# The mesh product written as three products of high and low parts, with its loads moved to ScalarE and its loops written out

## The chip, the cores and the metric

The kernel runs on one core of one Trainium2 chip. The metric is the device time of the whole program in microseconds (us), the median of several runs.

## What is computed

A node array of 1250 x 512 passes through a three-layer graph network with a residual norm, then through an edge and node network with a second norm. The change touches only one product inside the second network. There the edge network multiplies, for every edge, the concatenation of an edge embedding, the mesh features of the source node and the grid features of the target node by one weight of 1536 x 512:

```
e_in = jnp.concatenate([e, mesh_nfeat[src], grid_nfeat[dst]], axis=-1)
e_new = _mlp(e_in, edge_W0, edge_b0, edge_W1, edge_b1, edge_g, edge_beta) + e
```

The kernel does the middle third once per node and not once per edge: it computes `mesh_nfeat[0:1250] @ edge_W0[512:1024]` up front, stores the 1250 x 512 result in a table in device memory (`mesh_table`), and the edge stage later gathers rows of that table.

## The kernel before

The program has three parts with a barrier between the first two: `phase_a` (the first 325 us of the profile), `phase_b` (the layers of the first network; the edge stage is nested in it) and `phase_d` (the last norm). Only `phase_a` is touched. It runs, on TensorE and in this order:

1. transposes and products of weights (`turn_weight`, `jobs`, the vectors of L761 to L770), to about 104 us;
2. the mesh product (L772 to L796): the 1250 rows are ten tiles of 125 rows. `turn` (L772) transposes a tile of `mesh` through the identity into PSUM bank 4 or 5, ScalarE's `mesh_copy` (L661) copies it to `mesh_t`, `multiply` (L780) multiplies it by the weight `w0b` in plain float32 into bank 6 or 7, VectorE's `mesh_copy` (L562) copies the result to `mesh_out`, and the DMA queue of SyncE (SP) stores it. All buffers are double. The order on TensorE is turn, turn, multiply, multiply for a pair of tiles, the first pair written out, the other four in a hardware loop;
3. the first layer's products (L798 to L830): each tile of `h` is turned (`turn_h`), split into a high part (ScalarE, `high`) and a low part (VectorE, `low`), and multiplied in `product` (L70) by two weights that are split in the same way. `product` takes, for each of four chunks, three matmuls of float32r operands: high by high, high by low, low by high;
4. counting of edges per pair of nodes with one-hot matrices (L832 to L855), in 176 steps. VectorE makes the one-hot matrices (L596, L597). Each step is released by a gate: SP opens the even ones and GpSimd (POOL) the odd ones (`open_gates`, L269), both of them after a first increment from TensorE's queue at L850.

Other queues beside the mesh product: SP loads mesh tile n+2 when tile n has been turned (L330), stores finished tiles (L333), then loads a bias (L339), waits for all scatters of GpSimd (L341), loads the sorted pairs (L342) and the next weights. GpSimd sends 72 small scatters (L391, L395) and then 24 of another kind (L145) before it enters `open_gates`. VectorE turns the pairs into numbers in the tile NB - 3 = 7 of the first layer (L623 to L627). ScalarE splits the first layer's weights into `w_hi` between the first mesh tiles (L672), and VectorE makes `w_lo` (L572).

Of the kernel before, what the change touches and what calls it, by code (L numbers as in the profile page):

```python
# [25 lines left out]
F32 = mybir.dt.float32  # L26
F32R = mybir.dt.float32r
# [3 lines left out]
ALU = mybir.AluOpType  # L31
ACT = mybir.ActivationFunctionType
# [3 lines left out]
P = 128  # L36
N = 1250
E = 21250
D = 512
A4 = 4  # L40
KC = D // P
NB = 10
NPB = N // NB
# [74 lines left out]

SORT_AT, TEMP_AT, FOLD_AT, SBUF_END = 87296, 112128, 132864, 229344  # L120
SUMS_AT, LATE_AT, AGG_AT, U_AT, SPARE_AT = 24768, 90624, 104192, 179968, 220928

# [35 lines left out]
def phase_a(nc, ctx, t, scratch, keep):  # L159

    sort, temp, hot, fold = (Region(nc, at, end) for at, end in (
        (SORT_AT, TEMP_AT), (TEMP_AT, FOLD_AT), (TEMP_AT, FOLD_AT), (FOLD_AT, SBUF_END)))
# [56 lines left out]
    w1t = [fd(f"w1t_{i}", [P, KC, D]) for i in range(2)]  # L219
    w1gt = [fd(f"w1gt_{i}", [P, KC, D]) for i in range(2)]  # L220
    w0a, wnb, w0b = (fd(n, [P, KC, D]) for n in ("w0a", "wnb", "w0b"))
    jobs_out = [fd(f"jobs_out{i}", [P, D]) for i in range(2)]
    rows_out = [fd(f"rows_out{i}", [3, D]) for i in range(2)]
    mesh = [fd(f"mesh{i}", [NPB, D]) for i in range(2)]
    mesh_t = [fd(f"mesh_t{i}", [P, KC, P]) for i in range(2)]
    mesh_out = [fd(f"mesh_out{i}", [NPB, D]) for i in range(2)]

    h, w = keep["h"], [keep["w0"], keep["w1"]]
    w_hi, w_lo, hc, ht_hi, ht_lo = ([keep[f"{n}{i}"] for i in range(2)] for n in ("w_hi", "w_lo", "hc", "ht_hi", "ht_lo"))
    bias0, u_hi, u_lo = keep["bias0"], keep["u_hi"], keep["u_lo"]  # L230
# [23 lines left out]
    mesh_in = [sem(f"mesh_in{i}") for i in range(2)]  # L254
    mesh_stored = [sem(f"mesh_stored{i}") for i in range(2)]
    mesh_turned, mesh_t_ok, mesh_mm, mesh_ok = (sem(n) for n in ("mesh_turned", "mesh_t_ok", "mesh_mm", "mesh_ok"))
    hot_ok = sem("hot_ok")
    count_mm = [sem(f"count_mm{b}") for b in range(3)]
    copied_out = [sem(f"copied_out{b}") for b in range(3)]
# [6 lines left out]
    def spread(b):  # L266
        return b[:].rearrange("p (k n) -> p k n", k=KC)[:, :, 0:NPB]
# [30 lines left out]
    def _(sp):  # L298
# [25 lines left out]
            for m, name in enumerate(vectors[r][0]):  # L324
                sp.dma_start(rows(scratch[name]), rows_out[r % 2][m:m + 1, :]).then_inc(job_out[r % 2], 16)

        with sp.Fori(0, NB // 2 - 1) as i:
            for u in range(2):
                sp.wait_ge(mesh_turned, 2 * i + u + 1)
                move_rows(sp, mesh[u][:], node_rows(t["L1_gnn_mesh_nfeat"], 2 * i + 2 + u), mesh_in[u])  # L330
            for u in range(2):
                sp.wait_ge(mesh_ok, 2 * i + u + 1)
                move_rows(sp, node_rows(scratch["mesh_table"], 2 * i + u), mesh_out[u][:], mesh_stored[u])  # L333
        for u in range(2):
            n = NB - 2 + u
            sp.wait_ge(mesh_ok, n + 1)
            move_rows(sp, node_rows(scratch["mesh_table"], n), mesh_out[u][:], mesh_stored[u])
# [68 lines left out]
    def _(dve):  # L406
# [155 lines left out]
        def mesh_copy(n, u, fixed):  # L562
            if not fixed:
                dve.wait_ge(mesh_stored[u], (n - u) * (MOVED // 2))
            dve.wait_ge(mesh_mm, n + 1)
            dve.tensor_copy(mesh_out[u][:], bank[6 + u][0:NPB, :]).then_inc(mesh_ok, 1)

        for u in range(2):
            mesh_copy(u, u, True)
        for i in range(2):  # L570
            dve.wait_ge(w_hi_ok, i + 1)
            dve.tensor_tensor(w_lo[i][:], w[i][:], w_hi[i][:].bitcast(F32), ALU.subtract).then_inc(w_lo_ok, 1)  # L572
        with dve.Fori(1, NB // 2) as i:
            for u in range(2):
                mesh_copy(2 * i + u, u, False)

        def low(n):
            u = n % 2
# [26 lines left out]
        for n in range(NB):  # L605
            u = n % 2
# [26 lines left out]
    def _(act):  # L633
# [21 lines left out]
        for r in range(len(vectors)):  # L655
            act.wait_ge(job_mm, NJ + r + 1)
            act.wait_ge(job_out[r % 2], rows_stored(r % 2, r))
            m = len(vectors[r][0])
            act.activation(rows_out[r % 2][0:m, :], bank[r % 2][0:m, :], ACT.Copy).then_inc(row_out_ok, 1)

        def mesh_copy(n, u, fixed):  # L661
            if not fixed:
                act.wait_ge(mesh_mm, n - 1)
            act.wait_ge(mesh_turned, n + 1)
            act.activation(mesh_t[u][:, :, 0:NPB],
                           bank[4 + u][:].rearrange("p (k n) -> p k n", k=KC)[:, :, 0:NPB], ACT.Copy).then_inc(mesh_t_ok, 1)

        for u in range(2):
            mesh_copy(u, u, True)
        act.wait_ge(next_in, MOVED + 32)  # L670
        for i in range(2):
            act.activation(w_hi[i][:], w[i][:], ACT.Copy).then_inc(w_hi_ok, 1)  # L672

        def copy_h(n):
            if n >= 2:
# [3 lines left out]
        for n in range(2):  # L679
            copy_h(n)  # L680

        with act.Fori(1, NB // 2) as i:
            for u in range(2):
                mesh_copy(2 * i + u, u, False)

        def high(n):
            act.wait_ge(hc_turned, n + 1)
# [24 lines left out]
    def _(pe):  # L712
# [59 lines left out]
        def turn(n, u, fixed):  # L772
            pe.wait_ge(mesh_in[u], MOVED if fixed else (n - u) * (MOVED // 2) + MOVED)
            if not fixed:
                pe.wait_ge(mesh_t_ok, n - 1)
            for c in range(KC):
                last = pe.transpose(bank[4 + u][:, c * P:c * P + NPB], mesh[u][:, c * P:(c + 1) * P], k["ident"][0:NPB, 0:NPB])
            last.then_inc(mesh_turned, 1)

        def multiply(n, u, fixed):  # L780
            pe.wait_ge(mesh_t_ok, n + 1)
            if not fixed:
                pe.wait_ge(mesh_ok, n - 1)
# [6 lines left out]
        for u in range(2):  # L790
            multiply(u, u, True)
        with pe.Fori(1, NB // 2) as i:
            for u in range(2):
                turn(2 * i + u, u, False)
            for u in range(2):
                multiply(2 * i + u, u, False)  # L796

        def turn_h(n):  # L798
            pe.wait_ge(hc_ok, n + 1)
# [81 lines left out]
def node_rows(matrix, n):  # L881
    return matrix[n * NPB:(n + 1) * NPB, :] if isinstance(n, int) else matrix[ds(n * NPB, NPB), :]
# [1366 lines left out]
```

## Time and profile before

| | us |
|---|---|
| median of 3 runs | 2269.05 (2267.54 to 2270.96) |
| profiled execution, its own time | 2268.53 |
| its span, first to last instruction | 2266.8 |
| TensorE busy in the span | 2191.7 |
| mean granted TensorE clock | 0.991 of full speed |

Times inside the profile are counted from the start of the span. An engine's row in a timeline gives the start, how long the merged group took, engine, line, operation, output and inputs, shape, how many instructions, and in brackets how long the engine was idle before and who ended that. "SPq", "POOLq" and "PEldq" are the instruction queues of those engines, where waits, increments and DMA issues are handled; a queue can be ahead of its engine. `b_w_hi`, `b_ht_hi` and the like are the first layer's high and low parts.

### The profile page before, as it was taken

The numbers are of one execution on the slowest core, as the hardware profiler recorded it, in microseconds if no ns is written. First come the engines' busy times: TensorE is split into PE (matmuls) and PEld (weight loads), VectorE is DVE, ScalarE is ACT, GpSimd is POOL, SyncE is SP. The second block draws the span as 40 slices with busy tenths as digits, with TensorE's granted clock in tenths as the row PEclk, the third lists the DMA queues.
The fourth block names the chain that finished last, engine by engine and source line by source line (L and its number), as shares of the span: only waits on it lengthen the run. The fifth ranks groups of instructions, "written<-read, shape, count | busy, mean of one in ns | idle before, by whom it ended". The sixth has DMA issues, their size and how long they took to land. (4 is left out here: it accounts for less than half of the span.)

```text
span 2266.8 us, 44871 instructions
## 1 busy us (share of the span) xinstructions
PE 2191.7 (97%) x13036; PEld 1880.9 (83%) x13040; DVE 1502.4 (66%) x3372; ACT 1217.2 (54%) x2244; POOL 1207.9 (53%) x1725
## 2 busy tenths in 40 slices
PE   6999989999999999999999999999999999999898
PEld 4358877777789989989899898998989989889776
DVE  8325985343856776677767767667676776766666
ACT  1211114242346667666676677666767667667421
POOL 1785018884525555555555555555555565555223
PEclk9999999999999999999999999999999999999899
DMA  8231001112364333333233333333333323333131
GB/s 243 67 74 41 0 5 40 8 40 52 89 192 121 64 63 64 60 65 63 58 65 65 63 62 64 61 65 62 63 60 65 65 60 62 63 62 63 29 92 45
DMA packets 80400, 149.80 MB, mean 66 GB/s; under 512 B 20247, under 2 KB 20713, under 8 KB 80341
## 3 DMA queue, kind: packets, MB, share of 16 engines
q0 software_dynamic: 48464, 98.04, 22.7%
q1 hardware_dynamic: 31877, 51.01, 7.1%
q8 instruction: 33, 0.54, 0.1%
q14 instruction: 26, 0.21, 0.0%
HBM read 128.90 MB, written 19.71 MB: 66 GB/s over the span
## 5 line engine op out<-in xcount | busy, mean ns | idle before, releaser
L1655 ACT ACTIVATE b_bank<-c_bias 128x512 f32<-128x512 f32 x528 | 316.4, 599 | 15.1 <-PE b_bank L1767 5.2
L145 POOL DMA_INDIRECT s_attrs<-k_attrs,k_row_i x170 | 224.2, 1319 | 168.5 <-POOLq L2221 117.7
L1588 DVE CUSTOM_DVE_ANT_0 b_bank<-b_bank,c_p,k_floor 128x512 f32<-128x512 f32 x176 | 132.5, 753 | 255.6 <-PE b_bank L1789 254.7
L1433 POOL DMA_INDIRECT c_from_src<-s_dst_table,c_at_nodes x173 | 278.6, 1611 | 31.5 <-issue 31.5
L1844 PE MATMUL b_bank<-k_m_hi,c_pt_hi 128*128 128x512 f32 x704 | 293.8, 417 | 0.0
L1420 POOL DMA_INDIRECT c_from_src<-s_mesh_table,c_at_nodes x176 | 202.0, 1148 | 156.3 <-POOL c_at_nodes L1416 143.1
L1845 PE MATMUL b_bank<-k_m_lo,c_pt_hi 128*128 128x512 f32 x704 | 278.0, 395 | 0.0
L1846 PE MATMUL b_bank<-k_m_hi,c_pt_lo 128*128 128x512 f32 x704 | 273.9, 389 | 0.0
L1439 POOL TENSOR_TENSOR c_dev<-c_var,k_half 128x1 f32<-128x1 f32 x176 | 98.6, 560 | 327.4 <-DVE c_var L1570 327.4
L1726 ACT ACTIVATE c_h<-c_from_src 128x512 f32<-128x512 f32 x176 | 111.3, 632 | 263.4 <-DVE c_from_src L1609 263.4
L1787 PE MATMUL b_bank<-c_m_hi,c_ht_hi 128*128 128x384 f32 x704 | 222.5, 316 | 6.3 <-DVE c_ht_lo L1575 6.0
L1787 PE MATMUL b_bank<-k_m_hi,c_pt_hi 128*128 128x384 f32 x704 | 224.7, 319 | 0.0
L1789 PE MATMUL b_bank<-c_m_hi,c_ht_lo 128*128 128x384 f32 x704 | 218.6, 311 | 0.0
L1788 PE MATMUL b_bank<-c_m_lo,c_ht_hi 128*128 128x384 f32 x704 | 217.8, 309 | 0.0
L1789 PE MATMUL b_bank<-k_m_hi,c_pt_lo 128*128 128x384 f32 x704 | 217.1, 308 | 0.0
L1788 PE MATMUL b_bank<-k_m_lo,c_pt_hi 128*128 128x384 f32 x704 | 216.9, 308 | 0.0
L1604 DVE SCALAR_TENSOR_TENSOR c_rp_lo<-c_p,c_dev,c_rp_hi 128x512 fp32r<-128x512 f32 x176 | 132.3, 751 | 74.1 <-ACT c_rp_hi L1718 71.8
L1846 PEld LDWEIGHTS b_bank<-k_m_hi,c_pt_lo 128*128 128x128 f32 x704 | 132.8, 189 | 32.3
L1718 ACT ACTIVATE c_rp_hi<-c_p,c_dev 128x512 fp32r<-128x512 f32 x176 | 127.7, 726 | 55.0 <-POOL c_dev L1455 54.9
L1651 ACT ACTIVATE c_p<-b_bank 128x512 f32<-128x512 f32 x176 | 105.6, 600 | 92.4 <-PE b_bank L1764 91.8
L1844 PEld LDWEIGHTS b_bank<-k_m_hi,c_pt_hi 128*128 128x128 f32 x704 | 132.4, 188 | 23.9
L1455 POOL TENSOR_TENSOR c_dev<-c_var,k_half 128x1 f32<-128x1 f32 x176 | 130.1, 739 | 41.0 <-DVE c_var L1591 35.6
(355 smaller groups left out, 5862.8 us busy)
## 6 DMA issues: line engine op xcount, KB each, us to landing
c_from_src<-s_mesh_table,c_at_nodes POOLq DMA_INDIRECT x176
c_from_src<-s_dst_table,c_at_nodes POOLq DMA_INDIRECT x173, 4.7
s_attrs<-k_attrs,k_row_i POOLq DMA_INDIRECT x170
a_mesh<-in_L_gnn_mesh_nfeat_dram SPq DMA_DIRECT2D x10, 224.0 KB
k_h<-in_x_dram POOLq DMA_DIRECT2D x1, 2240.0 KB
s_mesh_table<-a_mesh_out SPq DMA_DIRECT2D x10, 224.0 KB
b_x<-in_x_dram SPq DMA_DIRECT2D x10, 224.0 KB
s_node_own<-b_out SPq DMA_DIRECT2D x10, 224.0 KB
```

What stands on the lines that cost most here:

```text
L145: return pool.indirect_dma_start(scratch["attrs"], bass.IndirectOffsetOnAxis(ap=k["row_i"][0:EP, c:c + 1], axis=0), k["attrs"][0:EP, A4 * ...
L1420: pool.indirect_dma_start(from_src[u][:], None, scratch["mesh_table"], bass.IndirectOffsetOnAxis(ap=at_nodes[u][:, 0:1], axis=0)).then_inc ...
L1433: pool.indirect_dma_start(from_src[u][:], None, scratch["dst_head" if head else "dst_table"], bass.IndirectOffsetOnAxis(ap=at_nodes[u][:, ...
L1588: dve.tensor_tensor_reduce(var1_bank[:], var1_bank[:], p[u % 2][:], 1.0 / D, k["floor"][:, 0:1], ALU.mult, ALU.add, var[u][:, 0:1]).then_i ...
L1604: dve.scalar_tensor_tensor(out=rp_lo[u][:], in0=p[u % 2][:], scalar=dev[u][:, 0:1], in1=rp_hi[u][:].bitcast(F32), op0=ALU.mult, op1=ALU.su ...
L1655: act.activation(bank[:], bias[:, m, :], ACT.Copy).then_inc(bank_set, 1)
L1787: pe.matmul(to, left[0][:, c, :], high, start=False, stop=False, skip_group_check=True)
L1788: pe.matmul(to, left[0][:, c, :], low, start=False, stop=False, skip_group_check=True)
L1789: last = pe.matmul(to, left[1][:, c, :], high, start=False, stop=(c == KC - 1), skip_group_check=True)
L1844: pe.matmul(edge_bank[:], left[0], m_hi[1][:, c, :], start=False, stop=False, skip_group_check=True)
L1845: pe.matmul(edge_bank[:], left[0], m_lo[1][:, c, :], start=False, stop=False, skip_group_check=True)
L1846: last = pe.matmul(edge_bank[:], left[1], m_hi[1][:, c, :], start=False, stop=(c == KC - 1), skip_group_check=True)
```

## The change

- `mesh_t` becomes float32r. `w0b` is split into `w0b_hi` (ScalarE, after the second vector) and `w0b_lo` (VectorE), and each turned tile gets a low part `mesh_lo` (VectorE, `mesh_low`). `w0b_hi` lies where `w0a` was, `w0b_lo` over `w0b` itself, `mesh_lo` over `wnb`.
- `multiply` uses `product`: twelve matmuls of float32r operands for a tile in place of float32 matmuls of four chunks.
- The order on TensorE becomes turn 0, turn 1, then for each n: multiply n, turn n+2, all of it written out.
- Mesh tiles 2 to 9 are loaded from ScalarE's queue (`mesh_load`), behind the copy of tile n-2. SP only stores.
- `w_hi` and `w_lo` are made between other tiles than before: ScalarE's `w_hi` behind the loads of tiles 3 and 4, VectorE's `w_lo` behind tiles 2 and 4.

```diff
-    mesh_t = [fd(f"mesh_t{i}", [P, KC, P]) for i in range(2)]
+    mesh_t = [fd(f"mesh_t{i}", [P, KC, P], F32R) for i in range(2)]
...
-        with sp.Fori(0, NB // 2 - 1) as i:
-            for u in range(2):
-                sp.wait_ge(mesh_turned, 2 * i + u + 1)
-                move_rows(sp, mesh[u][:], node_rows(t["L1_gnn_mesh_nfeat"], 2 * i + 2 + u), mesh_in[u])
-            for u in range(2):
-                sp.wait_ge(mesh_ok, 2 * i + u + 1)
-                move_rows(sp, node_rows(scratch["mesh_table"], 2 * i + u), mesh_out[u][:], mesh_stored[u])
...
+        for n in range(NB):
             sp.wait_ge(mesh_ok, n + 1)
+            move_rows(sp, node_rows(scratch["mesh_table"], n), mesh_out[n % 2][:], mesh_stored[n % 2])
...
+        def mesh_low(n, u, fixed):
+            dve.wait_ge(mesh_t_ok, n + 1)
+            if not fixed:
+                dve.wait_ge(mesh_mm, n - 1)
+            dve.tensor_tensor(mesh_lo[u][:, :, 0:NPB], spread(bank[4 + u]), mesh_t[u][:, :, 0:NPB].bitcast(F32),
+                              ALU.subtract).then_inc(mesh_lo_ok, 1)
+
+        dve.wait_ge(w0b_hi_ok, 1)
+        dve.tensor_tensor(w0b_lo[:], w0b[:], w0b_hi[:].bitcast(F32), ALU.subtract).then_inc(w0b_ok, 1)
         for u in range(2):
+            mesh_low(u, u, True)
+        for n in range(NB):
+            mesh_copy(n, n % 2, n < 2)
+            if n + 2 < NB:
+                mesh_low(n + 2, n % 2, False)
+            if n in (2, 4):
+                i = n // 2 - 1
+                dve.wait_ge(w_hi_ok, i + 1)
+                dve.tensor_tensor(w_lo[i][:], w[i][:], w_hi[i][:].bitcast(F32), ALU.subtract).then_inc(w_lo_ok, 1)
...
+            if r == 1:
+                act.activation(w0b_hi[:], w0b[:], ACT.Copy).then_inc(w0b_hi_ok, 1)
...
+        def mesh_load(n):
+            act.wait_ge(mesh_turned, n - 1)
+            move_rows(act, mesh[n % 2][:], node_rows(t["L1_gnn_mesh_nfeat"], n), mesh_in[n % 2])
+
         for u in range(2):
             mesh_copy(u, u, True)
+            mesh_load(2 + u)
         act.wait_ge(next_in, MOVED + 32)
         for i in range(2):
             act.activation(w_hi[i][:], w[i][:], ACT.Copy).then_inc(w_hi_ok, 1)
+            mesh_copy(2 + i, i, False)
+            mesh_load(4 + i)
...
+        for n in range(4, NB):
+            mesh_copy(n, n % 2, False)
+            if n + 2 < NB:
+                mesh_load(n + 2)
...
         def turn(n, u, fixed):
             pe.wait_ge(mesh_in[u], MOVED if fixed else (n - u) * (MOVED // 2) + MOVED)
             if not fixed:
-                pe.wait_ge(mesh_t_ok, n - 1)
+                pe.wait_ge(mesh_lo_ok, n - 1)
...
         def multiply(n, u, fixed):
-            pe.wait_ge(mesh_t_ok, n + 1)
-            if not fixed:
+            pe.wait_ge(mesh_lo_ok, n + 1)
+            if fixed:
+                pe.wait_ge(w0b_ok, 1)
+            else:
                 pe.wait_ge(mesh_ok, n - 1)
-            for c in range(KC):
-                last = pe.matmul(bank[6 + u][0:NPB, :], mesh_t[u][:, c, 0:NPB], w0b[:, c, :], start=(c == 0), stop=(c == KC - 1))
-            last.then_inc(mesh_mm, 1)
+            left = (lambda c: mesh_t[u][:, c, 0:NPB], lambda c: mesh_lo[u][:, c, 0:NPB])
+            product(pe, bank[6 + u][0:NPB, :], left, (lambda c: w0b_hi[:, c, :], lambda c: w0b_lo[:, c, :]),
+                    range(KC)).then_inc(mesh_mm, 1)
 
         for u in range(2):
             turn(u, u, True)
+        for n in range(NB):
+            multiply(n, n % 2, n < 2)
+            if n + 2 < NB:
+                turn(n + 2, n % 2, False)
```

## Rows read from the trace of the kernel before

**Rows 1.** Busy time by stretch: PE, PEld, DVE, ACT, POOL; clock, DMA share, GB/s.

```profile
104.00:145.20 41.20, 39.93 (x121) 19.24 (x121) 10.54 (x11) 10.55 (x15) 33.36 (x26) 1.00 0.43 108
207.20:323.60 116.40, 110.23 (x1939) 104.33 (x1938) 111.26 (x346) 13.78 (x38) 2.11 (x2) 1.00 0.01 1
```

**Rows 2.** TensorE's timeline, the mesh product and the start of the first layer.

```profile
103.95 1.07 PE L777 MATMUL a_bank<-k_ident,a_mesh 125*128 125x125 f32 x8
105.28 7.13 PE L785 MATMUL a_bank<-a_w0b,a_mesh_t 128*125 128x512 f32 x16 [0.26 <-issue]
112.25 1.02 PE L777 MATMUL a_bank<-k_ident,a_mesh 125*128 125x125 f32 x8
...
145.21 1.02 PE L803 MATMUL a_bank<-k_ident,b_hc 125*128 125x125 f32 x8
147.20 0.49 PE L73 MATMUL a_bank<-b_w_hi,b_ht_hi 128*125 128x512 f32 x1 [0.97 <-DVE b_ht_lo L582]
```

**Rows 3.** TensorE's timeline, one tile of the first layer (24 product matmuls, then a turn).

```profile
153.24 0.48 PE L73 MATMUL a_bank<-b_w_hi,b_ht_hi 128*125 128x512 f32 x1
...
158.45 0.39 PE L74 MATMUL a_bank<-b_w_lo,b_ht_hi 128*125 128x512 f32 x1
158.69 0.40 PE L75 MATMUL a_bank<-b_w_hi,b_ht_lo 128*125 128x512 f32 x1
...
159.27 0.48 PE L73 MATMUL a_bank<-b_w_hi,b_ht_hi 128*125 128x512 f32 x1
```

**Rows 4.** ScalarE's timeline around the mesh product.

```profile
97.19 0.59 ACT L659 ACTIVATE a_rows_out<-a_bank 2x512 f32<-2x512 f32 x1 [2.85 <-PE a_bank L769]
...
104.63 1.07 ACT L665 ACTIVATE a_mesh_t<-a_bank 128x500 f32<-128x500 f32 x2
105.58 3.71 ACT L672 ACTIVATE b_w_hi<-k_w 128x2048 fp32r<-128x2048 f32 x2
```

**Rows 5.** VectorE's timeline around the mesh product and in the first layer.

```profile
109.01 0.69 DVE L566 COPY a_mesh_out<-a_bank 125x512 f32<-125x512 f32 x1 [30.25 <-PE a_bank L785]
113.06 4.48 DVE L572 TENSOR_TENSOR b_w_lo<-k_w,b_w_hi 128x2048 fp32r<-128x2048 f32 x2
146.47 0.68 DVE L582 TENSOR_TENSOR b_ht_lo<-a_bank,b_ht_hi 128x500 fp32r<-128x500 f32 x1 [0.36 <-ACT b_ht_hi L690]
196.52 0.28 DVE L624 TENSOR_SCALAR a_pair_src<-a_pair_i 88x256 int32<-88x256 int32 x1
```

**Rows 6.** DMA issues on SP (ns min/median/max), then KB and us to landing.

```profile
L875 SPq DMA_DIRECT2D a_mesh<-in_L_gnn_mesh_nfeat_dram x20: 311/329/1922, 13.8 to 133.0; - x20
...
b_bias<-in_L_gnn_bs_dram SPq DMA_DIRECT2D x1, 256.0 KB, 3.8
a_w<-in_L_gnn_emb_W_dram SPq DMA_DIRECT2D x1, 1024.0 KB, 5.5
```

**Rows 7.** DMA traffic from 105.87 to 109.87 us, GB/s in 40 slices of 0.1 us.

```profile
GB/s 0 22 7 23 0 0 0 0 0 102 61 184 102 123 184 328 410 410 389 209 51 31 87 84 225 184 164 164 164 328 307 287 229 235 85 22 28 7 0 0
```

**Rows 8.** GpSimd's timeline while VectorE made w_lo.

```profile
111.67 1.18 POOL L391 DMA_INDIRECT s_pairs<-a_sort_pay,a_chunk_row  x1 [0.30 <-issue]
113.16 3.25 POOL L391 DMA_INDIRECT s_pairs<-a_sort_pay,a_chunk_row  x1 [0.30 <-issue]
116.71 1.89 POOL L391 DMA_INDIRECT s_pairs<-a_sort_pay,a_chunk_row  x1 [0.30 <-issue]
```

**Rows 9.** What can hold the count: pair load on SP, queues at the gates.

```profile
175.09 0.29 SPq L342 DMA_DIRECT2D a_pair_i<-s_pairs  x1
...
L273 POOLq MOVE  x1: 29/29/29, 191.7 to 191.7; - x1
...
L850 PEldq EVENT_SEMAPHORE  x3: 51/51/51, 204.4 to 204.7; - x3
```

**Rows 10.** Stretches in which the granted clock was low (columns as in the first group).

```profile
325.70:332.40 6.70, 3.59 (x9) 2.85 (x10) 2.12 (x9) 2.54 (x2) 4.13 (x4) 0.50 0.06 1
...
2254.00:2258.00 4.00, 3.84 (x10) 3.07 (x11) 2.29 (x5) 0.00 (x0) 2.53 (x3) 0.57 0.01 3
```

More of the change, by code:

```diff
@@ L120 @@
 SORT_AT, TEMP_AT, FOLD_AT, SBUF_END = 87296, 112128, 132864, 229344
+W0A_AT, WNB_AT, W0B_AT = (FOLD_AT + n * KC * D * 4 for n in (6, 7, 8))
 SUMS_AT, LATE_AT, AGG_AT, U_AT, SPARE_AT = 24768, 90624, 104192, 179968, 220928
@@ L221, in phase_a @@
     w0a, wnb, w0b = (fd(n, [P, KC, D]) for n in ("w0a", "wnb", "w0b"))
+    assert fold.at == W0B_AT + KC * D * 4
     jobs_out = [fd(f"jobs_out{i}", [P, D]) for i in range(2)]
@@ L224, in phase_a @@
     mesh = [fd(f"mesh{i}", [NPB, D]) for i in range(2)]
-    mesh_t = [fd(f"mesh_t{i}", [P, KC, P]) for i in range(2)]
+    mesh_t = [fd(f"mesh_t{i}", [P, KC, P], F32R) for i in range(2)]
     mesh_out = [fd(f"mesh_out{i}", [NPB, D]) for i in range(2)]
+    w0b_hi = Region(nc, W0A_AT, SBUF_END)("a_w0b_hi", [P, KC, D], F32R)
+    w0b_lo = Region(nc, W0B_AT, SBUF_END)("a_w0b_lo", [P, KC, D], F32R)
+    late_low = Region(nc, WNB_AT, SBUF_END)
+    mesh_lo = [late_low(f"a_mesh_lo{i}", [P, KC, P], F32R) for i in range(2)]
     h, w = keep["h"], [keep["w0"], keep["w1"]]
@@ L256, in phase_a @@
     mesh_turned, mesh_t_ok, mesh_mm, mesh_ok = (sem(n) for n in ("mesh_turned", "mesh_t_ok", "mesh_mm", "mesh_ok"))
+    w0b_hi_ok, w0b_ok, mesh_lo_ok = sem("w0b_hi_ok"), sem("w0b_ok"), sem("mesh_lo_ok")
     hot_ok = sem("hot_ok")
@@ L325, in _ @@
                 sp.dma_start(rows(scratch[name]), rows_out[r % 2][m:m + 1, :]).then_inc(job_out[r % 2], 16)
-        with sp.Fori(0, NB // 2 - 1) as i:
-            for u in range(2):
-                sp.wait_ge(mesh_turned, 2 * i + u + 1)
-                move_rows(sp, mesh[u][:], node_rows(t["L1_gnn_mesh_nfeat"], 2 * i + 2 + u), mesh_in[u])
-            for u in range(2):
-                sp.wait_ge(mesh_ok, 2 * i + u + 1)
-                move_rows(sp, node_rows(scratch["mesh_table"], 2 * i + u), mesh_out[u][:], mesh_stored[u])
-        for u in range(2):
-            n = NB - 2 + u
+        for n in range(NB):
             sp.wait_ge(mesh_ok, n + 1)
-            move_rows(sp, node_rows(scratch["mesh_table"], n), mesh_out[u][:], mesh_stored[u])
+            move_rows(sp, node_rows(scratch["mesh_table"], n), mesh_out[n % 2][:], mesh_stored[n % 2])
         sp.dma_start(bias0[:], rows(t["L0_gnn_bs"][0]).broadcast_to([P, D])).then_inc(bias_in, 16)
@@ L566, in mesh_copy @@
             dve.tensor_copy(mesh_out[u][:], bank[6 + u][0:NPB, :]).then_inc(mesh_ok, 1)
-        for u in range(2):
[L569 to L575, printed above, removed]
+        def mesh_low(n, u, fixed):
[6 more added lines that the diff above has]
+        dve.tensor_tensor(w0b_lo[:], w0b[:], w0b_hi[:].bitcast(F32), ALU.subtract).then_inc(w0b_ok, 1)
+        for u in range(2):
+            mesh_low(u, u, True)
[7 more added lines that the diff above has]
+                dve.tensor_tensor(w_lo[i][:], w[i][:], w_hi[i][:].bitcast(F32), ALU.subtract).then_inc(w_lo_ok, 1)
         def low(n):
@@ L680, in _ @@
             copy_h(n)
-        with act.Fori(1, NB // 2) as i:
-            for u in range(2):
-                mesh_copy(2 * i + u, u, False)
+        for n in range(4, NB):
+            mesh_copy(n, n % 2, False)
+            if n + 2 < NB:
+                mesh_load(n + 2)
         def high(n):
@@ L780, in multiply @@
         def multiply(n, u, fixed):
-            pe.wait_ge(mesh_t_ok, n + 1)
-            if not fixed:
+            pe.wait_ge(mesh_lo_ok, n + 1)
+            if fixed:
+                pe.wait_ge(w0b_ok, 1)
+            else:
                 pe.wait_ge(mesh_ok, n - 1)
-            for c in range(KC):
-                last = pe.matmul(bank[6 + u][0:NPB, :], mesh_t[u][:, c, 0:NPB], w0b[:, c, :], start=(c == 0), stop=(c == KC - 1))
-            last.then_inc(mesh_mm, 1)
+            left = (lambda c: mesh_t[u][:, c, 0:NPB], lambda c: mesh_lo[u][:, c, 0:NPB])
+            product(pe, bank[6 + u][0:NPB, :], left, (lambda c: w0b_hi[:, c, :], lambda c: w0b_lo[:, c, :]),
+                    range(KC)).then_inc(mesh_mm, 1)
         for u in range(2):
             turn(u, u, True)
[L790 to L796, printed above, removed]
+        for n in range(NB):
+            multiply(n, n % 2, n < 2)
+            if n + 2 < NB:
+                turn(n + 2, n % 2, False)
         def turn_h(n):
```

## The prediction

> **What bounds the kernel now.** I read the busy time by stretch first, because a share over the whole span hides which stage a change touches. The mesh stage lasts 41.2 us, of which TensorE is busy 39.93, and it is not busy with anything else [rows 1]. VectorE and ScalarE are busy about 10.5 us each, GpSimd 33.4 us with scatters that are not needed here. So TensorE's own work ends this stage. The timeline of TensorE says how it is spent: a pair of tiles repeats every 8.24 us (103.95 to 112.25 is the first, with four more behind it, to 145.21), of which two turns take about 1.0 and sixteen float32 matmuls 7.0; the idle time is 0.26 us a pair, one wait for the copy of the turned tile [rows 2]. The whole stage is 145.21 - 103.95 = 41.26 us. The chain of waits on the page reaches back only into the last part of the program, so it says nothing of this stage; what matters is what stands behind it. Behind it TensorE goes on at once with the first layer [rows 2], and it is busy 97% of the whole span. The queues are in order and the second part begins behind a barrier, so time taken out here is kept if no other queue has a date of its own before that barrier.
>
> **The change, part by part.**
>
> *The product.* Twelve float32r matmuls of 128*125 by 128x512 replace eight float32 ones. The first layer runs just this form: a tile there starts at 153.24 and the next at 159.27, 6.03 us for 24 matmuls and a turn; two neighbours start 0.233 us apart (158.45 to 158.69, rounded) [rows 3]. So 24 matmuls are 5.60 and a turn with its changes of form is 6.03 - 5.60 = 0.43. A mesh tile becomes 12 x 0.233 = 2.80, plus 0.43 for a turn, 3.23 us; before it was 8.24 / 2 = 4.12. In the first layer the operands are written by the same copies and subtractions, so I see no reason for another rate.
>
> *The start.* The chain turn, high part, low part, product is in the rows of the first layer: turn at 145.21, product at 147.20, 1.99 us [rows 2], and VectorE's part of it 0.68 [rows 5]. So the first mesh product starts at 103.95 + 1.99 = 105.94 where it started at 105.28. Then ten products, 28.0, and eight turns, 3.4: the stage ends at 137.4. The saving is 145.21 - 137.4 = 7.8 us.
>
> *The low parts.* `w0b_hi` is one more ScalarE copy of 128x2048: two take 3.71 us, so 1.86 [rows 4]. It starts behind the second vector's copy, at 97.19 + 0.59 = 97.8, and ends near 99.7; the next vector's copy comes 0.59 + 2.85 us after the second's, at 100.6 [rows 4]. `w0b_lo` is half of 4.48 us, 2.24 [rows 5], done by about 102; VectorE is otherwise idle for 30 us there [rows 5]. Both cost nothing; without that idle time the first product would start up to 4 us later. Each tile adds 0.68 for `mesh_low` to 0.69 for the copy out, 1.4 of 3.23 us on VectorE. The path from a turn to its low part is 1.5 us and lies behind the product of the tile before, 2.80 us, now that turn n+2 comes ahead of multiply n+1. `w_lo` is 2.24 us behind tiles 2 and 4: it makes the copy out of the next tile 0.8 us late, and the next low part is still ready 1.5 us before its product. Nothing.
>
> *The loads on ScalarE.* No row shows a DMA issued from ScalarE. Nearest are SP's mesh issues, 0.31 to 1.92 us, median 0.33; that is the same form of instruction on another queue [rows 6]. 1.92 is the end of a range of twenty whose median is 0.33, so I take 0.33: two issues and a copy are 0.66 + 0.55 = 1.2 us of 3.23, and ScalarE keeps up even with both `w_hi` (3.71) and two `hc` (a copy of 512 columns, 0.59 each) between the tiles, 4.9 us in all [rows 4]. Behind each issue on ScalarE stands the copy of the next turned tile, and for that copy VectorE's low part and the product wait.
>
> The load itself: two tiles, 512 KB, issued from 105.87 on, moved between 106.8 and 109.5 [rows 7], so one tile is in place about 2.5 us after its issue; a bias of 256 KB took 3.8, a weight of 1 MB 5.5 [rows 6]. Tile 2 is issued at 104.6 to 105.3 and wanted behind product 0, at 105.94 + 2.80 = 108.7: at 2.5 us it is early, at 3.8 it is 0.3 us late. Later loads are issued as soon as the tile before in the buffer has been turned and are wanted two tiles on: 2 x 3.23 - 0.43 - 0.66 = 5.4 us. I take nothing for the loads, and 0 to 1 us as the bound.
>
> The move alone gains nothing: SP has the time for its four issues in 3.23 us. By a rule of the Trainium skill ("DMA: Bandwidth & Descriptors", Issuing engines are not separate DMA queues), transfers from several issuing engines run on the same 16 DMA engines, and only issue time is saved. By that rule the sum is the same, since no issue time is on the path here.
>
> *GpSimd.* While VectorE made `w_lo`, two scatters took 3.25 and 1.89 us in place of 1.18: 2.8 us lost beside 4.48 us of VectorE [rows 8]. `w0b_lo` has the same form, so it should delay the scatters by about 1.4 us (bounds 0 and 2.24). The pairs are loaded at 175.09 and read by VectorE at 196.52, then 188.7 [rows 5, 9]; with 1.4 us of delay and a 256 KB landing time of 3.8, they are there at 180.3. The gates: GpSimd's queue reached its loop at 191.7, and what both gate queues wait for comes from TensorE's queue at 204.4, then 196.6 [rows 9]; 4.9 us later, and 1.4 us of delay leaves 3.5. So it costs nothing here. The Trainium skill ("SBUF — State Buffer", Who interferes with whom) states that a VectorE instruction with two SBUF inputs blocks a GpSimd one that reads SBUF, but infers that descriptor generation is left alone. By the first half the scatters are late, by the second they are not; the row shows them late, and the sum is the same with either.
>
> *Kept for last.* The written-out loops remove the loop branches, which show no idle time beyond 0.26 us a pair [rows 2]. The count paces itself: VectorE is busy 111.26 of 116.4 us, TensorE 110.23 [rows 1]; it starts earlier and lasts as long.
>
> *The clock.* The mesh stage and the first layer are at full clock (2.4 GHz) with the same short idle before the first product, so I count on that. After the count the granted clock was 0.50 for 6.7 us, and in the last 4 us 0.57 [rows 10]. About eight matmuls at 0.43 instead of 0.23 us cost 1.7 us in each. Where these stretches fall relative to the work is not set by the kernel, and the three runs spread over 3.4 us; I keep plus or minus 2 us.
>
> **Sum.** 2268.53 - 7.8 = 2260.7 for an execution like the profiled one. That one is 0.5 below the median of 2269.05, so 2261.2 for the median; I say 2261.
>
> **The rivals.**
>
> *Part of the gain is given back to the load's round trip* (8%). With two mesh buffers the period is half of turn, issue and landing; above 5.4 us of landing it stretches. For it: a 1 MB load took 5.5 [rows 6], and stores now come every 3.23 us. Against: 2.5 us for one of these tiles [rows 7]. At 6.9 us a tile takes (6.9 + 1.1) / 2 = 4.0, and eight tiles lose 8 x 0.75 = 6 us; the middle of this case is a loss of 3, 2264.
>
> *Little or no gain: GpSimd's gates* (5%). GpSimd's queue must reach its loop before TensorE's increment. From 4.9 us of delay on the first odd step waits, and at 12.7 us the gain is gone: 2268.5. What could do it is that the ten new low parts block GpSimd for their whole length as well: 2.24 + 6.8 = 9.0 us, 4.1 lost, 2265. For it are the two long scatters beside `w_lo` [rows 8]; against it is that these took 2.8 us for 4.48, and that a low part reads one operand from PSUM.
>
> *Slower: ScalarE becomes the bound* (4%). If an issue on its queue takes 1.92 us, SP's longest [rows 6], ScalarE needs 10 x 0.59 + 16 x 1.92 + 4.9 = 41.5 us from 104.63, so its last copy ends at 146.1, and low part and product follow, 149.6: 4.4 us later than 145.21, 2273.5. It binds against TensorE from 1.16 us an issue and against the kernel before from 1.64. Against: the median of 0.33.
>
> *It doesn't do what it says*: if the float32r matmuls ran at 0.43 us, a tile would be 5.6 us and the time 2283. The first layer speaks against that; below 1%.
>
> **How the numbers follow.** The full gain has 82%: 2261, with 2258.5 to 2263.5 as its own range. The range of 8 in 10 takes in the clock below and part of the round-trip case above: 2257 to 2265, a little wider below than the full gain's own because only three runs show the clock's spread. A difference counts as faster or slower from 0.2%, 4.5 us, which is about what a measurement of this kernel tells from no change. Faster takes the full gain but for its edge, and half of the round trip: 0.87. Same: 0.08, the rest of these and the gates. Slower: 0.05.
>
> **What would show it.** In the changed profile L777's first turn is still at about 104; the mesh matmuls start 0.233 us apart and a tile repeats every 3.23 us; the first turn of `h` starts near 137.4. Right for the loads: no idle time on TensorE that a mesh load ends. Right for GpSimd: its queue reaches the gates near 193, before TensorE's increment at 196.6. The stretch of low clock behind the count, at 325.7 before, comes some 8 us earlier [rows 10]. The prediction is wrong if the period is above 3.4 us, if ScalarE's copies come late behind issues, if the first count waits for GpSimd's gate, or if the stage behind the barrier starts 7.8 us earlier and the end does not.

## The result: slower by 0.4%, where faster was forecast

| kernel | median us | runs | ratio to before, 95% |
|---|---|---|---|
| before | 2269.5 | 6 | |
| changed, first measurement | 2278.2 (2277.3 to 2280.4) | 6 | 1.0039 (1.0026 to 1.0052) |
| changed, second | 2270.65 | 10 | 1.001 (1.000 to 1.002) |
| changed, third | 2270.45 | 11 | 1.0004 (0.9995 to 1.0014) |
| changed, one instruction more on SyncE | 2262.15 | 9 | 0.9968 (0.9957 to 0.9978) |
| the same again | 2262.5 | 6 | 0.9969 (0.9957 to 0.9981) |

Each of these was compared with runs of the kernel before that were measured beside it (medians 2268.2 to 2269.5). One of the nine times in the fifth line is 3607.27 us, at a granted clock of 0.556; the ratio is that of the other eight, whose median is 2261.8. The forecast was 2261 us, range 2257 to 2265, with 5% on slower. It failed: the changed kernel was 0.4% slower in its first measurement, and no faster than the kernel before in the other two. The gain that it named is there; two losses in another stage took it back, and only one of them came again. The two lines at the bottom are the changed kernel with the loss that came again taken away.

The changed kernel's first profiled execution took a span of 2275.6 us (2266.8 before) at a mean clock of 0.990. I read it in the order of the prediction. First the timeline of TensorE at the mesh product; a row gives start, length, engine, line, operation, count, and idle time before it with what ended it. Lines 73 to 75 are the three products, 797 the turn of a mesh tile, 822 that of `h`.

```profile
102.59 1.07 PE L797 MATMUL a_bank<-k_ident,a_mesh 125*128 125x125 f32 x8
104.63 0.50 PE L73 MATMUL a_bank<-a_w0b_hi,a_mesh_t 128*125 128x512 f32 x1 [0.97 <-issue]
104.97 0.39 PE L74 MATMUL a_bank<-a_w0b_lo,a_mesh_t 128*125 128x512 f32 x1
105.20 0.39 PE L75 MATMUL a_bank<-a_w0b_hi,a_mesh_lo 128*125 128x512 f32 x1
...
107.53 0.59 PE L797 MATMUL a_bank<-k_ident,a_mesh 125*128 125x125 f32 x4
...
136.14 1.02 PE L822 MATMUL a_bank<-k_ident,b_hc 125*128 125x125 f32 x8
```

Matmuls 0.233 us apart, as forecast; and from the first turn to the turn of `h` 136.14 - 102.59 = 33.55 us, where [rows 2] had 41.26. That is 7.7 us gained, 7.8 forecast. ScalarE's DMA issues (count, ns min/median/max, first and last start), then from the timeline VectorE's low part of the weight and the scatter of GpSimd beside it:

```profile
L894 ACTq DMA_DIRECT2D a_mesh<-in_L_gnn_mesh_nfeat_dram x16: 318/410/718, 103.3 to 124.7; - x16
```

```profile
98.25 2.29 DVE L575 TENSOR_TENSOR a_w0b_lo<-a_w0b,a_w0b_hi 128x2048 fp32r<-128x2048 f32 x1 [19.31 <-ACT a_w0b_hi L671]
...
98.47 3.13 POOL L390 DMA_INDIRECT s_pairs<-a_sort_pay,a_chunk_row  x1 [0.30 <-issue]
```

An issue on ScalarE is 0.41 us in the median, for which [rows 6] had lent 0.33; no load is late. The scatter is delayed, as [rows 8] had let expect.

Then the edge count. The columns are those of [rows 1]: the stretch, its length, busy time (and instructions) of PE, PEld, DVE, ACT, POOL, clock, DMA share, GB/s. The 176 steps of the count are tiles of edges, and they fall into ten buckets. A bucket ends when ScalarE copies its counts out of PSUM (L706, then L726), and its gates wait for the copy of the bucket before. Of the kernel before, first bucket and the other nine:

```profile
207.90:218.90 11.00, 10.54 (x186) 10.05 (x185) 9.61 (x31) 0.04 (x1) 1.41 (x2) 1.00 0.03 1
218.90:323.30 104.40, 98.80 (x1753) 93.85 (x1751) 100.99 (x316) 12.84 (x37) 0.00 (x0) 1.00 0.00 0
```

Of the changed one:

```profile
198.80:219.00 20.20, 14.46 (x184) 12.22 (x183) 11.02 (x32) 0.00 (x0) 11.00 (x10) 0.75 0.06 2
219.00:330.30 111.30, 104.78 (x1754) 95.34 (x1752) 102.42 (x316) 12.88 (x37) 0.00 (x0) 1.00 0.00 0
```

The same matmuls take 131.5 us in place of 115.4. The first bucket has lost 9.2 us (the first loss), the other nine 6.9 us (the second). With the stage's 7.7 us the sum is 16.1 - 7.7 = 8.4 us, and the profiled spans differ by 8.8. The 0.4 us between the two lie outside: in this execution the first turn stood 1.4 us earlier, and what stands behind the count took 1.8 us longer.

*The second loss in the rows.* Who waited, between 220 and 322 us (in total, times, longest), before:

```profile
PEld a_bank L842 <- SPq L277: 5.0, 15, 0.5
PE a_bank L842 <- SPq L277: 1.9, 5, 0.4
...
DVE a_hot_src L596 <- PE a_bank L845: 1.5, 6, 0.3
```

and after:

```profile
DVE a_hot_src L606 <- PE a_bank L864: 7.0, 15, 0.8
PEld a_bank L861 <- SPq L284: 5.9, 15, 0.5
PE a_bank L861 <- SPq L284: 3.4, 10, 0.4
```

VectorE, which hardly waited, now waits for TensorE, and TensorE for SyncE's queue: the gate loop. It runs once for two tiles. Its load of the bucket number, in the last stretch where no bucket changes (ns, first and last start), before and after:

```profile
L274 SPq TENSOR_LOAD <-k_tile_bucket x10: 267/270/274, 311.1 to 321.1; - x10
```

```profile
L281 SPq TENSOR_LOAD <-k_tile_bucket x10: 267/270/272, 316.8 to 328.6; - x10
```

Nine iterations took 10.0 us, 1.11 each; now 11.8, 1.31. VectorE starts a tile every 0.62 to 0.63 us when nothing holds it, 1.25 us for two (read off its timeline). So the loop was the faster by 0.14 us, and it is now the slower by 0.06. Over the 80 iterations of nine buckets that is 4.8 of the 6.9 us; the others go at the changes of bucket. I read them as the late loop catching up (waits of up to 0.8 us in the row of VectorE); no run takes them apart. Yet the loop's own code is not in the diff, and each instruction in it takes what it took (267 to 274 ns for the load).

*The first loss in the rows.* TensorE behind the count's start:

```profile
202.92 0.27 PE L861 MATMUL a_bank<-a_hot_dst,a_hot_src 128*128 128x128 bf16 x2 [0.50 <-issue]
203.66 0.27 PE L861 MATMUL a_bank<-a_hot_dst,a_hot_src 128*128 128x128 bf16 x2 [0.47 <-issue]
204.40 0.28 PE L861 MATMUL a_bank<-a_hot_dst,a_hot_src 128*128 128x128 bf16 x2 [0.46 <-issue]
...
210.14 1.25 PE L861 MATMUL a_bank<-a_hot_dst,a_hot_src 128*128 128x128 bf16 x10 [0.98 <-DVE a_hot_dst L607]
```

Mostly two matmuls every 0.73 us, for seven microseconds. It is not TensorE alone: the queues of SyncE and GpSimd take their next steps at the same moments (202.9, 204.4 and 205.1 us in all three, within 0.05). Ten matmuls then take 1.25 us where 0.72 is usual, because the granted clock fell inside the stall:

```profile
201.50:204.60 3.10, 1.09 (x8) 0.53 (x8) 0.06 (x1) 0.00 (x0) 2.49 (x3) 1.00 0.08 2
204.60:214.90 10.30, 6.71 (x57) 5.25 (x56) 5.51 (x15) 0.00 (x0) 6.42 (x6) 0.50 0.08 2
```

TensorE was busy for 1.09 of the 3.10 us before the clock went to 0.50 (1.2 GHz), and it stayed there for 10.3 us. All the while GpSimd scatters attributes, and its last scatter ends at 212.5. In the kernel before these ended at 209.6, 1.7 us behind the count's start.

### The profile page after: what moved, and what is told of

The parts are those of the page before. It is cut to its first block and busy times, and to the rows that moved or that the text cites. A ratio compares the mean times of both kernels' runs of the same rounds, so it can differ in the third digit from the quotient of the medians.

```text
span 2275.6 us, 44848 instructions
## 1 busy us (share of the span) xinstructions
PE 2194.2 (96%) x13079; PEld 1892.7 (83%) x13080; DVE 1516.0 (67%) x3383; ACT 1222.2 (54%) x2245; POOL 1218.9 (54%) x1725
```

## The experiments

Theories: A, SyncE's rewritten code, by its form or its place, slows its gate loop; B, that loop is slow from what others do; C, the scatters beside the count cause the first bucket's stall; D, the stall belongs to the first pass through the loops. What each run was expected to give stands ahead of its result.

**1. SyncE's stores in a loop** (changed kernel):

```diff
-        for n in range(NB):
-            sp.wait_ge(mesh_ok, n + 1)
-            move_rows(sp, node_rows(scratch["mesh_table"], n), mesh_out[n % 2][:], mesh_stored[n % 2])
+        with sp.Fori(0, NB // 2) as i:
+            for u in range(2):
+                sp.wait_ge(mesh_ok, 2 * i + u + 1)
+                move_rows(sp, node_rows(scratch["mesh_table"], 2 * i + u), mesh_out[u][:], mesh_stored[u])
```

> The changed kernel, but the mesh stores on SyncE stand in a hardware loop again (five turns of two tiles) and are not written out; nothing else differs. In the profile of the changed kernel the nine steady buckets of the edge count took 111.2 us, in the kernel before 104.4 us, and SyncE's loop that opens the gates took 1.31 us an iteration of two tiles beside 1.12 us. Theory A (the form or place of SyncE's code ahead of that loop slows the loop): iteration back to 1.12 us, steady buckets about 104.4 us, the whole about 7 us shorter than the changed kernel, so about 2271 us, near the kernel before. Theory B (the gates are late because the engines' timing against each other changed, whatever the code): iteration stays at 1.31 us, 2278 us. In both the loss in the first bucket (about 9 us between the count's start at 198.9 us and its first bucket at 219.0 us) stays.

2268.7 us. The opposite of theory A's forecast came out: the iteration stayed at 1.29 us and the nine buckets at 110 us, and it was the stall that went (first bucket ready at 209.9 us).

**2. SyncE written out** (kernel before):

```diff
-        with sp.Fori(0, NB // 2 - 1) as i:
+        for i in range(NB // 2 - 1):
```

> The kernel before, but SyncE's mesh loads and stores are written out in the same order instead of standing in a hardware loop. Theory A: SyncE's gate loop goes from 1.12 us towards 1.31 us an iteration and the count gets some 7 us longer, about 2276 us. Theory B: nothing moves, 2269 us. If the place and not the form matters, any value between 1.12 and 1.31 us can come out, since the code ahead of the loop is longer here than in either kernel.

2268.0 us, 0.9997 (0.9987 to 1.0006), iteration 1.11 us. The form by itself does nothing.

**3 and 4. Twelve early columns of attributes**, in the changed kernel and in that of run 1:

```diff
-ATTR_EARLY, ATTR_LATE, ATTR_PAIR = 24, 16, 4
+ATTR_EARLY, ATTR_LATE, ATTR_PAIR = 12, 16, 4
```

> The changed kernel, but GpSimd scatters 12 columns of attributes ahead of the count instead of 24; the other 12 go behind the barrier. In the changed kernel the last of the 24 ends at 212.5 us, 13.6 us after the count's start at 198.9 us, and TensorE's matmuls come one to three at a time every 0.73 us from 201.5 to 209 us. Theory C (the scatters or GpSimd's late entry into its gate loop hold up the count): with 12 they end at about 198 us, the stall goes and the first bucket's copy comes about 9 us earlier, near 210 us. Theory D (the stall belongs to the first pass of the engines through their loops, code fetched late, whatever GpSimd does): the stall stays at the count's start and the first bucket stays near 219 us. The 12 columns behind the barrier may cost up to 12 x 1.17 = 14 us there, so the whole is between 2269 and 2292 us; the verdict rests on the time of the first bucket in the profile.

> Both edits at once: the mesh stores in a hardware loop, and 12 columns scattered ahead of the count. If theories A and C hold both, the first bucket is ready near 210 us and the last one near 210 + 104.4 = 314 us (330.3 us in the changed kernel, 323.3 us in the one before), and the whole is 16 us shorter than the changed kernel less what the 12 late columns cost: 2262 to 2276 us. If neither holds the last bucket stays near 330 us.

2269.4 and 2268.1 us. In both the stall is gone (first bucket 9.8 us), which seemed to bear out C, but it had gone in run 1 too, with all 24 scatters in place. The iteration stayed at 1.30 and 1.29 us. The last buckets came at 318.6 and 321.9 us, neither at 314 nor at 330.

What was left was the place of SyncE's code. I counted the instructions that the trace has on SyncE's queue ahead of the load of the bucket, a loop's body once: 95 in the kernel before and in run 2 (1.11 us), 79 in the changed kernel and in run 3, 78 in runs 1 and 4 (1.29 to 1.31). By the starts in the trace 0.15 of the 0.19 us lie in two gaps between instructions (the rest is spread over four others, 0.02 us or less each): branch to next instruction 0.233 us for 0.164 in both slow forms, and between the 79th and the 80th instruction, which is ahead of the load where 79 stand before it (0.184 for 0.103) and behind the load where 78 do (0.394 for 0.311). Runs 5 to 8 move the loop.

**5. Two satisfied waits more** (changed kernel, behind the load of the bias):

```diff
+        for _ in range(2):
+            sp.wait_ge(pool_const, 10)
```

> The changed kernel with two waits added on SyncE, ahead of its gate loop, that are long satisfied; nothing else. In the three kernels with the slow gate loop the extra 0.17 to 0.19 us of an iteration lie in two gaps: behind the branch back, and beside the 79th instruction of SyncE's program (ahead of it in the changed kernel, behind it in the one with the stores in a loop, where the loop starts one instruction earlier). Theory A2 (the code has a boundary there, the loop lies across it, and every crossing costs): two instructions more put the whole loop behind it, the iteration falls from 1.31 to 1.12 us, the steady nine buckets from 111.2 to about 104.4 us. If the first bucket's stall goes too, which two other edits took away, the whole comes to about 2261 us; if that stays, 2270 us. Theory B (the loop is slow because of what the other engines do at that time): iteration stays at 1.29 to 1.31 us and the whole at 2269 to 2278 us.

**2262.15 us**, 0.9968 (0.9957 to 0.9978). The load of the bucket number:

```profile
L281 SPq TENSOR_LOAD <-k_tile_bucket x10: 267/270/273, 304.9 to 314.9; - x10
```

10.0 us for nine iterations again. B falls. The two waits went into one instruction (80 ahead of the load), so one instruction is worth 8 us against the changed kernel without the stall (runs 9 and 13).

**6 and 7. 240 and 244 waits** at the same place in the kernel before.

> The kernel before with 240 satisfied waits added on SyncE behind its mesh stores, where it is idle until 175 us; at about 0.07 us each they take 17 us of that. Its gate loop then starts 256 instructions after the place that it has in the changed kernel. Theory A2, with a boundary every 256 instructions: the loop lies across the next one, the iteration goes from 1.12 to about 1.31 us, and the unchanged kernel gets 6 to 7 us slower, about 2276 us. Without such a period, or by theory B: 1.12 us and 2269 us.

> As the last, with 244 waits in place of 240: the loop stands four instructions further, behind the supposed boundary. Theory A2: 1.12 us an iteration and 2269 us. If adding this many instructions costs by itself (they run into the loads that follow), it is as slow as the last one.

**8. Three waits** in the kernel of run 1.

> The changed kernel with the mesh stores in a hardware loop (its first bucket was ready at 209.9 us, its iteration 1.29 us) and three satisfied waits ahead of the gate loop. Theory A2: 1.12 us an iteration, first bucket near 210 us, last one near 315 us, the whole about 2262 to 2264 us, faster than the kernel before by 0.2 to 0.3%. Theory B: unchanged, 2268.7 us.

2269.1 us, 1.29 us: my count was off again. Three waits are one instruction more, 79 ahead of the load, which is just the place of the changed kernel.

**9. The changed kernel itself.**

> The changed kernel itself once more. All six of its times lay at 2277 to 2280 us, but three edits that touch nothing of the count's own code (stores in a loop, 12 fewer scatters, three waits) all gave 2268.7 to 2269.4 us with the first bucket's stall gone and SyncE's gate loop still slow. If the stall belongs to this exact program it is at 2278 us again; if it belongs to where that program was loaded or to the chip it ran on, it is near 2269 us.

2270.65 us. The stall was gone, the loop as slow. First bucket and the others:

```profile
199.60:210.90 11.30, 10.48 (x185) 9.90 (x184) 11.06 (x30) 0.01 (x1) 8.86 (x9) 1.00 0.09 3
210.90:322.20 111.30, 104.75 (x1755) 95.34 (x1752) 102.85 (x316) 12.92 (x37) 0.89 (x1) 1.00 0.00 0
```

Nine scatters ran beside this first bucket, ten beside the stalled one: 11.3 us against 20.2. In the profile of run 8 it was ten as well, and 11.3 us. So C and D as causes by themselves are both out, and runs 1 and 3 had not removed the stall; it had not come.

**10. 480 waits in the kernel before**: 240 instructions, 335 ahead of the load.

> The kernel before with 480 satisfied waits on SyncE behind its mesh stores. Two waits go into one instruction, as the traces of the last kernels show (240 waits added 120 instructions), so this is the test that the one with 240 was meant to be: the gate loop stands 256 instructions behind its place in the changed kernel, at 0.07 us each 17 us in SyncE's idle time. Theory A2 with a boundary every 256 instructions: about 1.31 us an iteration in place of 1.12 us and about 2276 us; a boundary at that one place alone, or theory B: 1.12 us and 2269 us.

**2277.07 us**, 1.0043 (1.0026 to 1.006), with none of the change in it. The waits, and the load of the bucket:

```profile
L341 SPq EVENT_SEMAPHORE  x239: 17/28/28, 147.6 to 162.4; - x120
...
L274 SPq TENSOR_LOAD <-k_tile_bucket x10: 267/270/275, 316.7 to 328.6; - x10
```

The waits end at 162.4 us, ahead of the pair load [rows 9]. Nine iterations take 11.9 us, and the count 330.3 - 208.1 = 122.2 us where it took 115.4. VectorE waits 7.0 us for TensorE, as in the changed kernel:

```profile
DVE a_hot_src L598 <- PE a_bank L847: 7.0, 14, 0.8
PEld a_bank L844 <- SPq L277: 5.9, 15, 0.5
PE a_bank L844 <- SPq L277: 3.4, 10, 0.4
```

This is the second loss made to order: slow at 78, 79 and 335 instructions, fast at 80, 95, 215 and 217. The Trainium skill ("Advanced Engine Details and Errata", ISA Cache) gives an engine's instruction cache as lines of 16 KB, which are 256 instructions; 335 - 79 = 256 agrees. That the loop pays in every iteration for where it lies is shown by the runs alone, 0.19 to 0.21 us here. That it lies across the border of two such lines is my reading: only one distance was tried, and a border every 32, 64 or 128 instructions would give the same seven results.

**11. Four waits** in the kernel of run 1, and **12. one wait** in the changed kernel.

> The mesh stores in a loop, and four waits, which are two instructions, ahead of the gate loop, so that its first instruction is the first one behind the boundary (with three waits, one instruction, the load of the bucket stood as in the changed kernel, and the iteration took 1.29 us). Theory A2: 1.12 us an iteration, the whole about 2262 us. Theory B: 2269 us.

> The changed kernel with one satisfied wait more on SyncE, which goes into an instruction that is there already, so nothing behind it is moved. By theory A2 it does not help: the iteration stays at 1.31 us, the whole at 2269 to 2278 us, against 2262 us with two waits (one instruction more). If the wait itself helps and not the place, it is at 2262 us too.

2262.5 us (0.9965 to 0.9984 in ratio, 1.11 us) and 2270.25 us (1.31 us). The wait that moves nothing does nothing; the one instruction that moves the loop wholly behind the border mends it, with either form of the stores.

**13 and 14. The changed kernel, and beside it the kernel of run 5**, called the twin from here on.

> The changed kernel once more, beside its two-wait twin on one chip. Its second measurement gave 2270.65 us with the stall of the first bucket gone and the slow gate loop still there. If the stall is rare it is at 2269 to 2271 us again, and 7 to 8.5 us above the twin; if this run shows 2277 us and more for it alone, the stall comes and goes with where the program lies.

> The changed kernel with two satisfied waits (one instruction) ahead of SyncE's gate loop, again, in more rounds: 2261 to 2264 us, 0.2 to 0.35% below the kernel before, if the loop's place is the whole of what was lost beside the stall.

2270.45 and 2262.5 us, 8 us apart. The twin's count:

```profile
200.60:211.90 11.30, 10.50 (x185) 9.91 (x184) 11.06 (x31) 0.00 (x0) 8.60 (x8) 1.00 0.08 2
211.90:316.40 104.50, 98.86 (x1754) 93.90 (x1752) 100.70 (x316) 12.91 (x37) 0.00 (x0) 1.00 0.00 1
```

115.8 us, against 115.4 in the kernel before. Its mesh stage, from first turn to turn of `h`:

```profile
104.40:137.90 33.50, 32.53 (x162) 26.22 (x161) 17.05 (x21) 11.47 (x15) 27.39 (x21) 1.00 0.51 132
```

**15. One fp32 product** in the twin (high and low parts are mixed, so its values are not the reference's):

```diff
-            product(pe, bank[6 + u][0:NPB, :], left, (lambda c: w0b_hi[:, c, :], lambda c: w0b_lo[:, c, :]),
-                    range(KC)).then_inc(mesh_mm, 1)
+            for c in range(KC):
+                x, y = (mesh_t[u], w0b_hi) if c < KC - 1 else (mesh_lo[u], w0b_lo)
+                x, y = x[:, c, 0:NPB].bitcast(F32), y[:, c, :].bitcast(F32)
+                last = pe.matmul(bank[6 + u][0:NPB, :], x, y, start=(c == 0), stop=(c == KC - 1))
+            last.then_inc(mesh_mm, 1)
```

> The twin with two waits, but the mesh product is one fp32 product of four chunks again; it takes high parts in three chunks and low parts in one, so its values are not those of the reference, while the order, the loads, the low parts and their waits all stay. It tells what the three products alone are worth: fp32 took 35.7 us for ten tiles in the kernel before, three products 28.0 us as worked out in the prediction. If TensorE sets the period, each tile is 0.77 us longer and the whole 7 to 8 us longer, about 2270 us. If the loads or the low parts set it, less.

2270.0 us, 7.5 above the twin. TensorE:

```profile
114.23 0.59 PE L799 MATMUL a_bank<-k_ident,a_mesh 125*128 125x125 f32 x4
114.66 2.74 PE L811 MATMUL a_bank<-a_w0b_hi,a_mesh_t 128*125 128x512 f32 x6
117.24 1.02 PE L811 MATMUL a_bank<-a_w0b_lo,a_mesh_lo 128*125 128x512 f32 x2
118.10 0.59 PE L799 MATMUL a_bank<-k_ident,a_mesh 125*128 125x125 f32 x4
```

A tile takes 3.87 us, 0.64 more than 3.23, without idle time: 6.4 us of the 7.5 for ten tiles. The expectation had 0.77.

**16. The mesh loads back on SyncE** (changed kernel; 95 instructions ahead of the load of the bucket):

```diff
         for n in range(NB):
+            if n + 2 < NB:
+                sp.wait_ge(mesh_turned, n + 1)
+                move_rows(sp, mesh[n % 2][:], node_rows(t["L1_gnn_mesh_nfeat"], n + 2), mesh_in[n % 2])
             sp.wait_ge(mesh_ok, n + 1)
...
-            mesh_load(2 + u)
...
-            mesh_load(4 + i)
...
-            if n + 2 < NB:
-                mesh_load(n + 2)
```

> The changed kernel with the mesh loads back on SyncE, each ahead of the store two tiles earlier; 24 instructions more stand ahead of the gate loop, so it is clear of the boundary (1.12 us an iteration). The load of tile n+4 then queues behind the store of tile n+1: that is out some 4.7 us behind turn n+2 (3.2 us of work, 0.8 us of copy, 0.6 us of issues), and a load takes 1.9 us more to land, about 6.6 us against two periods of 6.46 us. If that is so the period grows by 0.1 to 0.4 us a tile and the whole by 1 to 3 us over the twin's 2262 us; if ScalarE's place for the loads is worth nothing it stays at 2262 us.

2269.0 us, 6.5 above the twin, where 1 to 3 were expected. TensorE, then SyncE's issues:

```profile
113.90 0.65 PE L796 MATMUL a_bank<-k_ident,a_mesh 125*128 125x125 f32 x4 [1.55 <-DMA a_mesh<-in_L_gnn_mesh_nfeat_dram]
...
122.29 0.65 PE L796 MATMUL a_bank<-k_ident,a_mesh 125*128 125x125 f32 x4 [1.68 <-DMA a_mesh<-in_L_gnn_mesh_nfeat_dram]
```

```profile
109.87 0.76 SPq L893 DMA_DIRECT2D s_mesh_table<-a_mesh_out  x2
110.68 0.80 SPq L893 DMA_DIRECT2D a_mesh<-in_L_gnn_mesh_nfeat_dram  x2
```

The turn of tile 3 waits for its load until 113.90 us. Its buffer was free from about 105 us, but the issue stood behind the store of tile 0, until 110.68, and the tile was in place 3.2 us later, where the expectation had counted 1.9. This pair of tiles takes 8.39 us, more than the 8.24 of [rows 2], and the stage 41.4 us, 7.9 more than in the twin. An order in which SyncE issues the load of tile 3 ahead of the store of tile 0 was not run.

## Why the prediction was wrong

*Product, start, low parts*: right. 0.233 us a matmul, 3.23 us a tile, 2.04 us to the first product (1.99 forecast) and 33.5 us for the stage, in each profile of the changed kernel, 7.7 us gained. Run 15 prices the products at 6.4 of these.

*Loads on ScalarE*: right that they cost nothing; 0.33 us an issue was 0.41. "The move alone gains nothing" holds by run 15, which has the move without the products, 2270.0 us. Its reason, "SP has the time for its four issues", was wrong. SyncE has the time but not the order: run 16 shows 6.5 us lost without the move. With these orders of issues the gain needs both edits together, and either alone stays near 2269 to 2270 us.

*GpSimd*: right for the gates, with less to spare than forecast. The scatter beside `w0b_lo` was 1.9 us late (3.13 for 1.19, forecast 1.4), the two beside `w_lo` took 2.38 and 3.16 us (3.25 and 1.89 before), and its queue reached the gates at 194.4 us, 2.7 us later than before. The first gates opened at 195.4, so 1.0 us was left of the 3.5 forecast. In the count itself the scatters do cost something, which the prediction left out. The count now starts while they still run: with all 24 columns ahead of the barrier, 4 to 10 of them ran beside the first bucket in the profiles of the changed kernel and its variants 1, 5, 8, 11 and 12, and 0 to 2 in those of the kernel before. VectorE's second instruction of a tile takes longer then (run 9):

```profile
203.76 0.57 DVE L607 TENSOR_SCALAR a_hot_dst<-a_dst_grid,k_dst_t 128x128 bf16<-128x128 int16 x1
...
213.33 0.25 DVE L607 TENSOR_SCALAR a_hot_dst<-a_dst_grid,k_dst_t 128x128 bf16<-128x128 int16 x1
```

Its mean is 0.42 us up to the end of the last scatter and 0.25 behind it. With eight or more scatters beside it and no stall the first bucket takes 11.3 us; with none, in runs 3 and 4, 9.8, as in runs 2, 6, 7, 10 and 16, where it starts late. Only the profile of the kernel before, 11.0 us with two scatters beside it, does not fit.

*Kept for last*: this is the step that failed. "The count paces itself", so that "it starts earlier and lasts as long", was put at nothing in the sum; in the first measurement the count lasted 16.1 us longer, of which the loop's place is 6.9 and the stall the rest. The step was read from busy times of VectorE and TensorE [rows 1], and the third partner, the two gate queues, was asked only when they arrive [rows 9], not how fast they turn. A row of the kernel before has it: 1.11 us an iteration against VectorE's 1.25. With 0.14 us of slack in a loop that it did not list, "lasts as long" is a claim that needed a bound above, and the diff shortened the code ahead of that loop from 95 instructions to 79. The nine buckets lasted 6.9 us longer by the loop's place, shown by runs 5, 10, 11 and 12 from both sides. None of the rivals was this one: the 4% on slower had ScalarE's issues as their cause, and these cost nothing.

*The first bucket's stall* is the other 8 us of the first measurement: 2278.2 against 2270.5. All six of those times are 2277 us or more, none of the 21 later ones of the same kernel is (the highest, 2276.4, is the third profile, with a late first turn and no stall), and no other profile has the stall. The program was the same, so something outside it had a part; where it was loaded and the chip would be such things, and the record cannot tell them apart. The scatters run beside it in both cases, so they are not enough by themselves; whether they are needed was not shown. Its cause stays open. It falls into the same step, "lasts as long", but no row of the kernel before could have told of it.

*The sum*: 2261 for 2262.15 and 2262.5 in the twin. The forecast for the work was right to 1.5 us; the forecast for the program was not. Against the kernels before measured beside them, runs 5, 11 and 14 gained 7.0, 5.7 and 6.2 us, where the stage gained 7.7. Up to 1.5 us of the gap is the first bucket beside the scatters; the rest is not told apart from the spread of the times.

The first turn of the changed kernel stood at 102.6, 103.3 and 110.3 us in its three profiles, so a single execution's span (2275.6, 2267.9, 2274.7) says little at this size. I compared stages from their own first instruction, and medians.

## What to carry to other kernels

A short hardware loop on a queue that paces others has a price for where it lies in the program: if an edit anywhere ahead of it, on the same engine, changes the instruction count, read its time per iteration again, and try one instruction more. When a stage is said to be unchanged, list every queue that turns once per step in it, with its time per iteration and its slack, the register loops too, which the busy shares leave out. When a stage starts earlier, ask what it then runs beside. And a load that queues behind a store waits for the product that the store waits for, however idle the queue is.

## What was not expected of the hardware

- SyncE's loop of nine instructions took 1.11 us an iteration with 80, 95, 215 or 217 instructions ahead of its second one, and 1.29 to 1.32 us with 78, 79 or 335.
- Two waits in a row on SyncE can become one instruction: 480 waits were 240 instructions, 0.062 us apart (14.8 us for 239).
- VectorE's `hot_dst` instruction (128x128) took 0.42 us in the mean while GpSimd scattered and 0.25 us behind the last scatter (run 9).
- In the one profile with the stall, TensorE's matmuls came mostly two at a time every 0.73 us for 7 us, in step with the queues of SyncE and GpSimd, VectorE stood still for 3.75 and 2.95 us, and the clock fell to 0.50 within the stall, from 204.6 to 214.9 us.
